# Key spreading on ScalarE, later and smaller query-weight products on GpSimd, and another row for the maxima, in a chain of four cross-attention layers

## The chip, the cores and the metric

The kernel runs on one core of a Trainium2 chip. The metric is the device time of one execution in microseconds. Engines are called by the profile's short names: PE (TensorE matmuls), PEld (its weight loads), DVE (VectorE), ACT (ScalarE), POOL (GpSimd), SP (SyncE, which only issues DMAs here).

## The reference, cut to what matters

Four cross-attention layers follow each other on a residual stream of width 256. The layer called 0 takes the context (4 x 64 tokens) as its latents and x (4 x 256 tokens) as the other side; the output of each layer is the x of the next.

```python
x = _L0_xattn_ref(ctx, x, mask_ik0, q_w, q_b, kv_w, kv_b, out_w, out_b, postnorm_w, mlp_w1, ...)  # 16 heads of 16, then an MLP
x = _L1_xattn_ref(x, ctx, mask_ff0, Wq, bq, Wk, bk, Wv, bv, Wo, bo, gamma, beta)                  # 32 query heads of 8, 8 key heads
x = _L2_xattn_ref(x, ctx, ctx, ...)   # two attentions, 16 heads of 128, one more (bias) key each, then an MLP
x = _L3_xattn_ref(x, ctx, mask_bf1, ...)  # 16 heads of 16, then an MLP

# one attention of layer 2
h = _layer_norm(x, ln_scale, ln_offset)
qh = (h @ wq + bq).reshape(b, q_len, 16, 128)
kh, vh = ctx @ wk + bk, ctx @ wv + bv          # and one bias row each behind them
weights = softmax(einsum('bqhk,bthk->bhqt', qh, kh) / sqrt(128))
x = x + einsum('bhqt,bthk->bqhk', weights, vh).reshape(b, q_len, 2048) @ wo + bo
```

In the text the layers are counted from 0, and the kernel's names carry that number (`kT1`, `kbd3`). "The second layer" of the change's short description is layer 1, "the second half" is the second attention of layer 2.

## The kernel before, in words

The program is written by hand, one instruction stream for each engine, with semaphores between them. An engine runs its stream in the order of the lines. A tile in PSUM comes from a ring (`wide`, three of 1024 columns; `narrow`, two of 512); PE waits for a tile to be drained, and the draining engine waits for it to be full.

*Layer 0* runs in 32 steps over eight groups of (batch, half of the width). Queries and keys are rounded into a high and a low part and stored to DRAM, and come back as `qrow` and `krow`, in which 48 rows hold the parts of one head, at partitions 0 and 64. Row `MASK_ROW` (48) carries the mask. `max_scores0` (L643) computes scores over `MAX_ROW` rows, DVE takes their maxima (L1536), PE turns them (L601), ACT negates them into `maxrow`, and two DMAs on ACT's queue (L1174) put them into row `MAX_ROW` of `qrow`, at partitions 49 and 113. The final scores (L662) then contract over `MAX_ROW + 1` rows, so the maximum is subtracted inside the matmul; row `MAX_ROW` of `krow` holds ones, which SP copies at the start from a row of `qrow` that stays one. The rows between are zero in `krow` and one in `qrow` from the memsets at the start.

*The MLPs* (`mlp` on PE, ACT and DVE) work in two halves of 512 tokens. PE makes four "up" tiles for a half (L507), ACT applies the Gelu to each in two instructions of 512 columns (L1142), DVE rounds it (L1440) and subtracts (L1441) for a high and a low part, and the "down" matmuls (L526) take all of them. In the order of PE, the down matmuls of the first half stand behind the first up tile of the second half. They run over six of the eight hidden chunks for two token blocks first and then wait for the rest.

*Layer 1* needs its keys as a block diagonal: `spread_keys(1, kT1, kbd1, head8, 16)` on POOL multiplies the keys, repeated for 16 heads, by a mask `head8` (one where the partition belongs to the head), in two instructions of 4096 elements per partition (L1782). It stands in POOL's stream behind the folded biases and in front of the wait for the last down tile of layer 0's MLP. PE's first `scores1` waits for `kbd_ready` 2. Layer 3 does the same with `kbd3`, 2 x 2048 elements, while DVE spreads the values into `vpad3` (L1692) and the MLP of layer 2 starts.

*Layer 2* folds queries and keys together. For each attention `precompute2` runs over 16 heads. DVE splits the key and value weights of a head (L1590, `kv_low`, behind ACT's rounded copy L1295), PE multiplies them with the context (L818), ACT evacuates, PE forms `G` with the query weights (L846) and, every second head, the products with the output weights (L859); L826 sums the bias values. The query weights arrive in eight groups of four heads, four for each attention. `multiply_wq(n)` on POOL multiplies a group by the norm's offset into `wprod` (L1765) and by the norm's scale in place (L1766), 1024 elements each; `query_shift(n)` on DVE sums `wprod` (L1617) and adds the bias (L1618); `shift_wq` on ACT adds that to the weights (L1303), waiting for `qshift_ready` at the first head of a group. Of the second attention's groups (4 to 7) POOL does 4 and 5 inside the first attention (steps 4 and 5 of `attend`), and 6 and 7 right behind it; DVE does `query_shift` 4 and 5 in steps 5 and 6, and 6 and 7 at heads 6 and 10 of the second precompute.

In an attention (`attend2`), for each block of 128 tokens PE makes scores (L876), DVE the maxima and sums, ACT the exponentials, POOL divides (`normalize`, L1754), PE turns the probabilities (L557) and applies the values (L898); DVE adds the residual (L1412), which frees PE's narrow tile, and takes the statistics, POOL the reciprocal root (L1732), DVE the normalization (L1392).

Of the kernel before, what the change touches and what calls it, by code (L numbers as in the profile page):

```python
# [19 lines left out]
MASK_ROW, MAX_ROW = 48, 49  # L20
# [80 lines left out]
def build(nc, t, out):  # L101
    ctx = ExitStack()
    with ctx:
# [849 lines left out]
        def _(sp):  # L953
# [55 lines left out]
            for i, lo, hi in ((0, 2 * T, KROW), (0, 0, T), (1, T, KROW)):  # L1009
                k0 = 64 * i + MAX_ROW  # L1010
                sp.dma_start(krow[k0:k0 + 1].rearrange("p a r n -> p (a r) n")[:, :, lo:hi].bitcast(F32),
                             qrow[P - 1:P, 0].rearrange("p r n -> p (r n)")[:, 0:hi - lo].unsqueeze(1).broadcast_to([1, 3 * PAIRS0, hi - lo]).bitcast(F32)
                             ).then_inc(ones_loaded, 16)
# [75 lines left out]
        def _(act):  # L1089
# [37 lines left out]

            def mlp(n, func, b1, turned):
# [4 lines left out]
                for half in range(2):  # L1133
                    for fp in range(NF // 2):
# [13 lines left out]
                        if i == TURN_UP[n]:  # L1148
                            norm_turned(*turned, (1,))

# [215 lines left out]
        def _(dve):  # L1366
# [271 lines left out]
            def precompute2(a):  # L1638
                for h in range(H2):
# [6 lines left out]
                    if a == 0 and 3 <= h < 3 + NQ:  # L1646
                        dve.wait_ge(x2_ready, h - 2)
                        stat(2, h - 3)
                    if h in (6, 10):
                        query_shift(4 * a + h // GROUP + 1)  # L1650
# [11 lines left out]
            def attend2(a, rows_before):  # L1662
                u0 = base["2a" if a == 0 else "2b"]
                for step in range(-3, NQ + 3):
# [4 lines left out]
                    if a == 0 and step in (5, 6):  # L1669
                        query_shift(step - 1)  # L1670
# [39 lines left out]
        def _(pool):  # L1710
# [46 lines left out]
            def multiply_wq(n):  # L1757
# [7 lines left out]
                link(g.tensor_tensor(wprod[:, n % 2], wq, offset, ALU.mult))  # L1765
                g.tensor_tensor(wq, wq, scale, ALU.mult).then_inc(wq_multiplied, 1)  # L1766
# [12 lines left out]
            def spread_keys(layer, kT, kbd, mask, heads_):  # L1779
                pool.wait_ge(*wide.empty(("k", layer)))  # L1780
                for c in range(NC):
                    g.tensor_tensor(kbd[:, c],  # L1782
                                    kT[:, c, :].rearrange("p (b k) -> p b k", b=B).unsqueeze(2).broadcast_to([P, B, heads_, T]),
                                    mask[:].unsqueeze(1).unsqueeze(3).broadcast_to([P, B, heads_, T]), ALU.mult
                                    ).then_inc(kbd_ready, 1)
# [53 lines left out]
            spread_keys(1, kT1, kbd1, head8, 16)  # L1839

# [20 lines left out]
            def between2(a):  # L1861
                def each(step):
# [6 lines left out]
                    if a == 0 and step in (4, 5):  # L1869
                        multiply_wq(step)  # L1870
# [12 lines left out]
            multiply_wq(6)  # L1883
            multiply_wq(7)
# [48 lines left out]
```

## Time and profile before

| | us |
|---|---|
| median of the 3 runs shown | 770.53 |
| lowest, highest | 766.96, 774.74 |
| the profiled execution's own time | 768.64 |
| its span, first to last instruction | 766.9 |
| PE busy in the span | 681.7 |
| DVE busy | 500.1 |
| ACT busy | 350.6 |
| POOL busy | 330.0 |

The profile is of one execution; all rows below are of it. Busy time of PE is not PE at its peak, since matmuls are pipelined and their ends are modelled. The granted clock (PEclk) is a mean over a stretch, 1.00 being the upper one of its two levels (2.4 GHz) and 0.50 the lower (1.2 GHz); over the whole span it is 0.942. In the timelines neighbouring instructions of one form are merged.

### The profile page before, as it was taken

How to read it: one execution, taken by the hardware profiler on the slowest of the kernel's cores; microseconds unless marked ns; L12 is line 12 of the kernel's file. 1: busy time of each engine (PE TensorE's matmuls, PEld its weight loads, DVE VectorE, ACT ScalarE, POOL GpSimd, SP SyncE). 2: the span in 40 equal slices, each digit the busy share in tenths (PEclk: the TensorE clock that was granted, in tenths of full speed). 3: DMA queues.
4: the chain of work that ended last, by engine and by line, in shares of the span. 5: the costliest groups of instructions: out<-in, count | busy, mean ns of one | idle time of the engine just before them, and what ended most of it. 6: DMA issues, size and time to landing. Idle time of an engine off the chain costs nothing.

```text
span 766.9 us, 11612 instructions
## 1 busy us (share of the span) xinstructions
PE 681.7 (89%) x4260; PEld 484.9 (63%) x4260; DVE 500.1 (65%) x844; ACT 350.6 (46%) x931; POOL 330.0 (43%) x288
## 2 busy tenths in 40 slices
PE   8789989998898798689999988999997998787798
PEld 6565556456793454467746766774675896345688
DVE  4446567557649999657556785445587874697543
ACT  2144444344114777456657434655661412585311
POOL 5033264533806989475225553003446222485100
PEclk9868899699999999899999999999998999996899
DMA  6955576000006000063330002230000003000000
GB/s 190 247 146 149 160 184 152 2 2 27 1 1 219 1 1 1 1 198 106 111 109 1 1 0 81 85 110 1 2 0 1 1 1 109 1 1 0 1 28 28
DMA packets 41009, 47.23 MB, mean 62 GB/s; under 512 B 5793, under 2 KB 35066, under 8 KB 40954
## 3 DMA queue, kind: packets, MB, share of 16 engines
q1 hardware_dynamic: 39784, 45.47, 19.9%
q10 hardware_dynamic: 1170, 1.02, 0.6%
q8 instruction: 35, 0.57, 0.3%
q14 instruction: 20, 0.16, 0.1%
HBM read 38.24 MB, written 8.13 MB: 60 GB/s over the span
## 4 chain that ended last, share of the span: by engine, by line
PE 57%; DVE 28%; ACT 4%; issue 4%; POOL 4%; DMA 3%; ACTq 0%; SPq 0%; DVEq 0%; POOLq 0%
PE narrow_ps L526 8%; PE wide_ps L876 6%; PE wide_ps L818 6%; PE wide_ps L507 5%; PE narrow_ps L707 4%; PE wide_ps L859 4%; PE narrow_ps L898 4%; DVE mx L1460 3%; DVE scoresb L1456 3%; PE wide_ps L846 3%; PE wide_ps L557 2%; DVE sums L1480 2%; DVE xn L1392 2%; PE wide_ps L643 2%; DVE hidden L1441 2%
## 5 line engine op out<-in xcount | busy, mean ns | idle before, releaser
L1732 POOL TENSOR_TENSOR rstd<-veps,mhalf 128x1 f32<-128x1 f32 x56 | 33.1, 591 | 161.9 <-DVE veps L1384 155.8
L1754 POOL TENSOR_TENSOR probs<-scoresb,rcp 128x1024 f32<-128x1024 f32 x40 | 78.8, 1969 | 28.3 <-DVE rcp L1485 28.3
L1096 ACT ACTIVATE probsT<-wide_ps 128x1024 f32<-128x1024 f32 x40 | 41.1, 1027 | 71.8 <-PE wide_ps L557 71.8
L526 PE MATMUL narrow_ps<-wstream_r,hidden 128*128 128x256 f32 x576 | 71.1, 284 | 2.8 <-DVE hidden L1441 2.5
L526 PEld LDWEIGHTS narrow_ps<-wstream_r,hidden 128*128 128x128 f32 x576 | 70.4, 191 | 3.8 <-DVE hidden L1441 2.7
L507 PE MATMUL wide_ps<-xq_r,wstream_r 128*128 128x512 f32 x192 | 64.0, 416 | 8.3 <-issue 8.0
L557 PEld LDWEIGHTS wide_ps<-ident,probs 128*128 128x128 f32 x320 | 39.8, 152 | 47.8 <-issue 47.4
L557 PE MATMUL wide_ps<-ident,probs 128*128 128x128 f32 x320 | 46.5, 294 | 26.2 <-POOL probs L1754 26.2
L1536 DVE TENSOR_REDUCE mx<-wide_ps 128x2 f32<-128x640 f32 x64 | 49.4, 817 | 27.4 <-PE wide_ps L643 27.2
L818 PE MATMUL wide_ps<-scoresb_r,probs_r 128*128 128x256 f32 x256 | 54.4, 295 | 8.2 <-DVE wstream_r L1590 5.8
L1728 POOL TENSOR_TENSOR xB<-xB,rows 128x256 f32<-128x256 f32 x40 | 30.2, 764 | 72.9 <-DVE rows L1659 72.2
L1142 ACT ACTIVATE scoresb<-wide_ps,col 128x512 f32<-128x512 f32 x48 | 30.4, 685 | 66.8 <-PE wide_ps L507 66.8
L898 PE MATMUL narrow_ps<-region,probsT 128*128 128x256 f32 x256 | 57.8, 380 | 1.6 <-DVE xB L1412 1.6
L876 PE MATMUL wide_ps<-region,actT 128*128 128x512 f32 x128 | 57.3, 595 | 1.4 <-ACT scoresb L1222 1.4
L818 PEld LDWEIGHTS wide_ps<-scoresb_r,probs_r 128*128 128x128 f32 x256 | 41.7, 189 | 18.9 <-issue 12.6
L898 PEld LDWEIGHTS narrow_ps<-region,probsT 128*128 128x128 f32 x256 | 47.5, 190 | 7.7 <-DVE xB L1412 1.8
L1590 DVE TENSOR_TENSOR wstream_r<-wstream,probs_r 128x256 fp32r<-128x256 f32 x64 | 32.7, 555 | 29.9 <-ACT probs_r L1295 29.9
L507 PEld LDWEIGHTS wide_ps<-xq_r,wstream_r 128*128 128x128 f32 x192 | 37.9, 202 | 17.1 <-issue 9.6
L1745 POOL TENSOR_TENSOR scoresb<-scoresb,mx 128x768 f32<-128x768 f32 x24 | 36.8, 1534 | 26.6 <-DVE negmx L1461 26.4
L1222 ACT ACTIVATE scoresb<-wide_ps,negmx 128x64 f32<-128x64 f32 x128 | 39.1, 334 | 12.7 <-DVE negmx L1471 12.5
L1412 DVE TENSOR_TENSOR xB<-narrow_ps,xB 128x256 f32<-128x256 f32 x48 | 20.1, 419 | 35.8 <-PE narrow_ps L526 23.6
L876 PEld LDWEIGHTS wide_ps<-region,actT 128*128 128x128 f32 x128 | 23.8, 190 | 28.9 <-issue 23.9
(195 smaller groups left out, 1599.2 us busy)
## 6 DMA issues: line engine op xcount, KB each, us to landing
wstream<-in_L_xattn_wk SPq DMA_DIRECT2D x8, 512.0 KB, 3.9
wstream<-in_L_xattn_wv SPq DMA_DIRECT2D x8, 512.0 KB, 5.0
wstream<-in_L_xattn_wo SPq DMA_DIRECT2D x8, 512.0 KB, 4.1
qrow<-qscratch SPq DMA_DIRECT2D x16, 192.0 KB
xq<-in_wqT SPq DMA_DIRECT2D x6, 512.0 KB, 5.2
kscratch<-kparts SPq DMA_DIRECT2D x8, 320.0 KB, 2.5
qscratch<-qparts SPq DMA_DIRECT2D x8, 256.0 KB, 3.5
wstream<-in_L_xattn_mlp_w SPq DMA_DIRECT2D x4, 512.0 KB, 4.4
```

What stands on the lines that cost most here:

```text
L507: m = mm(ps[:, j * 512:(j + 1) * 512], w1[pw][:, kc, f * P:(f + 1) * P], xparts[px][:, kc, half * 512:(half + 1) * 512], start=kc == 0 and ...
L526: m = mm(ps[:, 0:D], hidden[:, ph, f, qoff((q + i) % 4)], w2[pw][:, f, :], start=f == 0 and part == 0, stop=f == NF - 1 and part == 2)
L557: m = nc.tensor.transpose(ps[:, j * P:(j + 1) * P], probs[:, u % 2, j * P:(j + 1) * P], ident[:])
L818: last = mm(ps[:, m * 256:(m + 1) * 256], w[:, m, kc, :], cparts[:, part, kc, :], start=kc == 0 and i == 0, stop=kc == NC - 1 and i == 2)
L876: m = mm(ps[:, g * 512:(g + 1) * 512], actT[:, c, qoff(q)], G[:, c, 8 * g:8 * g + 8, b * T:(b + 1) * T], start=c == 0, stop=c == NC - 1)
L898: m = mm(ps[:, 0:D], probsT[:, u % 2, r * P:(r + 1) * P], VW[:, q // 2, r, :], start=r == 0, stop=r == 7)
L1096: nc.scalar.activation(dst, src, ACT.Identity, **kw).then_inc(ring.drained[ring.slot(key)], 1)
L1222: ins = nc.scalar.activation(scoresb[:, u % 3, h * T:(h + 1) * T], wide_ps[:, wide.slot(key), h * T:(h + 1) * T], ACT.Exp, scale=SCALE2, b ...
L1536: v.tensor_reduce(mx0[:, half % 2, qh, pl:pl + 3:2], ps[:, :, 0:KEYS0], AX, ALU.max).then_inc(wide.drained[wide.slot(key)], 1)
L1732: g.tensor_tensor(rstd[:, q:q + 1], veps[:, q:q + 1], mhalf[:], ALU.pow).then_inc(rstd_ready, 1)
L1745: g.tensor_tensor(s3[:, DIRECT:], s3[:, DIRECT:], mx[:, u % 3, DIRECT:].unsqueeze(2).broadcast_to([P, 16 - DIRECT, T]), ALU.subtract).then ...
L1754: g.tensor_tensor(probs[:, u % 2, :].rearrange("p (h k) -> p h k", h=16), s3, rcp[:, u % 3, :].unsqueeze(2).broadcast_to([P, 16, T]), ALU. ...
```

## The change

Four edits are made together.

- The keys of layer 1 are spread by ACT: `spread_keys1(part)` runs in the first MLP behind each of the eight up tiles, and each call issues four ACTIVATEs (Identity with a per-partition scale, a column of `head8`) of 256 elements, one for each (half of the width, head). POOL's `spread_keys(1, ...)` goes. Parts 3 and 7 increment `kbd_ready`.
- `multiply_wq(5)` on POOL moves from step 5 of the first attention to behind it; groups 5, 6 and 7 are multiplied in eight instructions of 256 elements each instead of two of 1024; groups 6 and 7 wait for the tile `G` of heads 1 and 4 of the second precompute. `query_shift(5)` on DVE moves from step 6 of the first attention to head 2 of the second precompute.
- The spreading of layer 3's keys on POOL is done batch by batch, in eight instructions of 512 elements instead of two of 2048.
- `MAX_ROW` is 63 instead of 49, so the two matmuls over these rows contract over 63 and 64 rows, the DMAs write partitions 63 and 127, and the ones are copied from partition 126.

```diff
-MASK_ROW, MAX_ROW = 48, 49
+MASK_ROW, MAX_ROW = 48, 63
...
-                             qrow[P - 1:P, 0].rearrange("p r n -> p (r n)")[:, 0:hi - lo].unsqueeze(1).broadcast_to([1, 3 * PAIRS0, hi - lo]).bitcast(F32)
+                             qrow[P - 2:P - 1, 0].rearrange("p r n -> p (r n)")[:, 0:hi - lo].unsqueeze(1).broadcast_to([1, 3 * PAIRS0, hi - lo]).bitcast(F32)
...
+            def spread_keys1(part):
+
+                if part == 0:
+                    act.wait_ge(wk_ready, NC)
+                for n in range(4 * part, 4 * part + 4):
+                    c, h = divmod(n, 16)
+                    last = nc.scalar.activation(kbd1[:, c, :, h, :], kT1[:, c, :].rearrange("p (b k) -> p b k", b=B),
+                                                ACT.Identity, scale=head8[:, h:h + 1])
+                if part % 4 == 3:
+                    last.then_inc(kbd_ready, 1)
+
             def mlp(n, func, b1, turned):
...
                         if i == TURN_UP[n]:
                             norm_turned(*turned, (1,))
+                        if n == 0:
+                            spread_keys1(i)
...
                     if a == 0 and 3 <= h < 3 + NQ:
                         dve.wait_ge(x2_ready, h - 2)
                         stat(2, h - 3)
+                    if a == 1 and h == 2:
+                        query_shift(5)
...
-                    if a == 0 and step in (5, 6):
-                        query_shift(step - 1)
+                    if a == 0 and step == 5:
+                        query_shift(4)
...
                 wq = wq2[n]
-                link(g.tensor_tensor(wprod[:, n % 2], wq, offset, ALU.mult))
-                g.tensor_tensor(wq, wq, scale, ALU.mult).then_inc(wq_multiplied, 1)
+                size = 1 if n >= 5 else GROUP
+                for h in range(0, GROUP, size):
+                    last = g.tensor_tensor(wprod[:, n % 2, h:h + size], wq[:, h:h + size], offset[:, 0:size], ALU.mult)
+                link(last)
+                for h in range(0, GROUP, size):
+                    last = g.tensor_tensor(wq[:, h:h + size], wq[:, h:h + size], scale[:, 0:size], ALU.mult)
+                last.then_inc(wq_multiplied, 1)
...
                 for c in range(NC):
-                    g.tensor_tensor(kbd[:, c],
-                                    kT[:, c, :].rearrange("p (b k) -> p b k", b=B).unsqueeze(2).broadcast_to([P, B, heads_, T]),
-                                    mask[:].unsqueeze(1).unsqueeze(3).broadcast_to([P, B, heads_, T]), ALU.mult
-                                    ).then_inc(kbd_ready, 1)
+                    for b in range(B):
+                        last = g.tensor_tensor(kbd[:, c, b],
+                                               kT[:, c, b * T:(b + 1) * T].unsqueeze(1).broadcast_to([P, heads_, T]),
+                                               mask[:].unsqueeze(2).broadcast_to([P, heads_, T]), ALU.mult)
+                    last.then_inc(kbd_ready, 1)
...
-            spread_keys(1, kT1, kbd1, head8, 16)
...
-                    if a == 0 and step in (4, 5):
+                    if a == 0 and step == 4:
                         multiply_wq(step)
...
             attend(base["2a"], NQ, 3, done2, None, between2(0), False)
-            multiply_wq(6)
-            multiply_wq(7)
+            for n in range(5, 8):
+                if n > 5:
+                    pool.wait_ge(*wide.full(("G", 1, 3 * n - 17)))
+                multiply_wq(n)
             attend(base["2b"], NQ, 4, done2, "L2_b_fc2", between2(1), False)
```

## Rows read from the trace of the kernel before

**Rows 1.** The page: span of the profiled execution.

```profile
span 766.9 us, 11612 instructions
```

**Rows 2.** DVE timeline, first MLP: start us, us, engine, line, operation, out<-in, forms.

```profile
185.64 1.22 DVE L1441 TENSOR_TENSOR hidden<-scoresb,hidden 128x1024 fp32r<-128x1024 f32 x1
...
193.85 7.97 DVE L1441 TENSOR_TENSOR hidden<-scoresb,hidden 128x1024 fp32r<-128x1024 f32 x1
```

**Rows 3.** Line 1782: instructions, ns least/median/most, first to last start us, forms.

```profile
L1782 POOL TENSOR_TENSOR region<-headbuf,head x2: 7401/7724/8048, 193.3 to 200.7; 128x4096 f32<-128x4096 f32 x2
L1782 POOL TENSOR_TENSOR region<-kT,head x2: 3618/3663/3708, 592.1 to 595.7; 128x2048 f32<-128x2048 f32 x2
```

**Rows 4.** PE timeline, same stage; brackets: idle before it, and the releaser.

```profile
194.91 4.47 PE L526 MATMUL narrow_ps<-wstream_r,hidden 128*128 128x256 f32 x36
201.88 7.52 PE L526 MATMUL narrow_ps<-wstream_r,hidden 128*128 128x256 f32 x60 [2.50 <-DVE hidden L1441]
```

**Rows 5.** ACT timeline, same stage.

```profile
185.57 1.26 ACT L1142 ACTIVATE scoresb<-wide_ps,col 128x512 f32<-128x512 f32 x2 [0.53 <-PE wide_ps L507]
```

**Rows 6.** ACT timeline, start of layer 2's second precompute.

```profile
455.95 0.84 ACT L1096 ACTIVATE headbuf<-wide_ps,col 128x256 f32<-128x256 f32 x2 [6.38 <-PE wide_ps L818]
456.68 0.51 ACT L1303 ACTIVATE xq<-xq,qshift 128x256 f32<-128x256 f32 x1
```

**Rows 7.** POOL timeline, first attention of layer 2 and behind it.

```profile
439.09 2.38 POOL L1765 TENSOR_TENSOR wprod<-xq,rows 128x1024 f32<-128x1024 f32 x1
...
456.88 2.41 POOL L1765 TENSOR_TENSOR wprod<-xq,rows 128x1024 f32<-128x1024 f32 x1
```

**Rows 8.** DVE timeline, same stages.

```profile
439.07 2.55 DVE L1392 TENSOR_SCALAR xn<-xB,mv,rstd 128x256 f32<-128x256 f32 x1
...
446.21 0.40 DVE L1392 TENSOR_SCALAR xn<-xB,mv,rstd 128x256 f32<-128x256 f32 x1
...
456.95 2.49 DVE L1392 TENSOR_SCALAR xn<-xB,mv,rstd 128x256 f32<-128x256 f32 x1 [0.66 <-POOL rstd L1732]
...
462.78 4.52 DVE L1590 TENSOR_TENSOR wstream_r<-wstream,probs_r 128x256 fp32r<-128x256 f32 x2
```

**Rows 9.** PE timeline, same stages.

```profile
442.01 3.72 PE L898 MATMUL narrow_ps<-region,probsT 128*128 128x256 f32 x16 [1.58 <-DVE xB L1412]
446.42 1.06 PE L557 MATMUL wide_ps<-ident,probs 128*128 128x128 f32 x8 [0.69 <-POOL probs L1754]
...
462.41 0.35 PE L818 MATMUL wide_ps<-scoresb_r,probs_r 128*128 128x256 f32 x1 [2.99 <-DVE wstream_r L1590]
```

**Rows 10.** The chain that ended last, second precompute: start us, us, what.

```profile
464.19 1.71 PE wide_ps L846 x4
465.90 1.01 PE narrow_ps L826 x8
...
473.19 0.87 PE wide_ps L846 x4
...
481.59 0.57 PE narrow_ps L826 x8
```

**Rows 11.** Groups of POOL, 385 to 480: busy us, mean ns, idle before.

```profile
L1728 POOL TENSOR_TENSOR xB<-xB,rows 128x256 f32<-128x256 f32 x8 | 5.6, 726 | 18.0 <-DVE rows L1659 18.0
```

**Rows 12.** Line 1692: DVE copies beside the spreading of layer 3's keys.

```profile
L1692 DVE COPY region<-v x8: 218/224/3635, 592.2 to 600.7; 64x128 f32<-64x128 f32 x8
```

**Rows 13.** Line 1609: DVE copies beside the first two groups of query weights.

```profile
L1609 DVE COPY region<-v x16: 186/192/2455, 231.2 to 243.0; 64x64 f32<-64x64 f32 x16
```

**Rows 14.** PE timeline, MLP of layer 2.

```profile
606.73 0.50 PE L507 MATMUL wide_ps<-actT_r,wstream_r 128*128 128x512 f32 x1 [0.15 <-DVE actT_r L1426]
```

**Rows 15.** Stretches of layer 0: busy by engine, PEclk, DMA share, GB/s.

```profile
40.00:60.00 20.00, 17.73 (x80) 12.66 (x78) 9.04 (x13) 6.99 (x15) 5.74 (x5) 0.60 0.54 151
...
140.00:155.00 15.00, 14.61 (x103) 7.09 (x103) 6.67 (x8) 4.61 (x10) 6.38 (x5) 0.56 0.01 2
```

**Rows 16.** Waits, 20 to 165: who waited for whom, us, times, longest.

```profile
PE wide_ps L662 <- DMA qrow<-maxrow: 0.6, 1, 0.6
```

## What the rows make of the change: the prediction

> **What bounds the kernel now.** The profiled execution has a span of 766.9 us [rows 1] and a time of 768.64 us, so 1.74 us lie around the span; the median of the runs shown is 770.53 us, 1.89 above it, and those runs spread from 766.96 to 774.74. I read first the page's chain that ended last, which is mostly TensorE with VectorE in second place, and then the stages in which the change acts: the timelines of POOL, DVE, PE and ACT side by side. What the reader is to see there is one pattern. A DVE instruction that reads and writes SBUF and starts beside a POOL tensor instruction ends when that POOL instruction ends. The MLP's subtraction takes 1.22 us alone, and 7.97 us when it starts half a microsecond behind the first of POOL's two key-spreading instructions of 7.4 to 8.0 us [rows 2, 3]. The normalization L1392 takes 0.40 us alone, 2.55 and 2.49 us beside a `multiply_wq` half of 2.4 us [rows 7, 8]. It matters only where PE then runs dry, and the PE timeline says where.
>
> **The change, part by part.**
>
> *A. Layer 1's keys go from POOL to ACT.* POOL loses 15.4 us in the first MLP [rows 3]. DVE's subtraction then ends near 193.85 + 1.22 = 195.07 instead of 201.82. PE had finished what it could do without it at 194.91 + 4.47 = 199.38 and stood 2.50 us for it [rows 4]. That wait goes, and PE is next limited by its own matmuls: **2.5 us**. What is late next is ACT. It gets 32 ACTIVATEs of 256 elements. A pair of that size takes 0.84 us out of PSUM, one alone in SBUF 0.51 [rows 6], so a group of four costs 1.7 to 2.0 us and eight groups 13.4 to 16.3 us. They sit behind the Gelu pairs of 1.26 us; ACT still waited 0.53 us for PE at the third [rows 5]. Following the order of the lines I get the third pair about 1 us late and the fourth under 0.5, both estimates. The cover is the gap between 195.07 and PE's need at 199.38: 4.3 us. If all three groups in front of the fourth pair stood in the open (6.1 us), 1.8 us of it would reach PE and A would be worth 0.7; nothing in the ACT timeline points there. In the second half of the MLP ACT has nothing but the Gelus. Later, `scores1` waits for `kbd_ready`; ACT's last increment comes with the last Gelu, before the last down matmuls of the MLP, so it costs nothing. POOL's clearing of `region` and its first two `multiply_wq` hang on the end of the MLP as before and move with it.
>
> *B1. `multiply_wq(5)` and `query_shift(5)` leave the first attention.* POOL's two instructions from 439.09 on hold DVE's normalization for 2.55 us where 0.40 is its own [rows 7, 8]. The residual addition behind it frees a PSUM slot that PE waits 1.58 us for, and 4.4 us later PE waits another 0.69 us for POOL's probabilities [rows 9]. Taking the first wait alone gives 1.58, both 2.27. Of the second part stays, since the last `normalize` still needs the last sums: **2.0 us**.
>
> *B2. The same work in pieces, in the second half of the precompute.* Today `multiply_wq(6)` starts at 456.88, 0.07 us before the last normalization, and the four instructions follow each other; behind it are held the normalization (2.49 us) and both pairs of weight splits, the second for 4.52 us [rows 7, 8]. PE stands 2.99 us for the first pair [rows 9], and the matmuls behind that wait run as at the lower clock level: the next four L846 take 1.71 us against 0.87 in a later group, the next eight L826 1.01 against 0.57 [rows 10]. That is 0.84 + 0.44 = 1.28 us on top. After the change POOL runs `multiply_wq(5)` here, eight pieces; a POOL instruction of 256 elements takes 0.73 us [rows 11], so 5.8 us instead of 4.8. It is due only at the fifth head, when ACT wants `qshift_ready` 6, long after. DVE now waits at most 0.73 us per instruction instead of 2.4. From below: normalization and one pair, three instructions, each behind a whole piece, 2.2 us, leave 2.99 - 2.2 = 0.8 us and no clock gain. From above: 2.99 + 1.28 = 4.27 us. I take a value near the upper end, because DVE's chain runs ahead of PE's next need by then, less 0.5 us (an estimate, part of one 0.73 us piece) for `multiply_wq(6)`, which now starts after the second head and meets the split for the fifth: **3.7 us**. `multiply_wq(7)` starts after the fifth head and is due at the eleventh; POOL has nothing else to do there, so both cost nothing. `query_shift(5)` becomes two DVE instructions behind the third head; the queue behind them, the next splits, is ahead of PE. No DMA is issued or moved.
>
> *C. Layer 3's keys in eight pieces of 512 instead of two of 2048.* By their own rate a piece takes 3.66 / 4 = 0.92 us [rows 3]; by the 256-wide instruction twice 0.73 = 1.45 [rows 11]. DVE has eight copies beside them, two held 3.6 us, the others 0.22 free [rows 12]. In the stage after the first MLP, where four POOL instructions follow each other, only a few of sixteen copies are held, but each for a whole instruction, up to 2.46 us [rows 13]: pieces that follow without a break pass the block on from copy to copy. Eight copies behind eight pieces end after 7.4 to 11.6 us, against 2 x 3.64 + 6 x 0.22 = 8.6 today. PE's only wait that comes from it is 0.15 us [rows 14]. So the ends are +0.15 and -3.0; I take **0.1 us**, by the instruction's own rate.
>
> *D. The row of the maxima.* Partition 49 becomes 63, and the contractions of L643 and L662 take 63 and 64 rows instead of 49 and 50. The added rows are zeros times ones, and the column counts stay, so no instruction is added: **0**, with two rivals below.
>
> Sum: 2.5 + 2.0 + 3.7 + 0.1 = 8.3 us. Against the profiled execution's own time that is 768.64 - 8.3 = 760.3, against the median 762.2; I say **761**. The bounds of the terms give 0.7 + 1.58 + 0.8 - 3.0 = 0.1 us at worst and 2.5 + 2.27 + 4.27 + 0.15 = 9.2 us at best.
>
> **Rivals.**
>
> *The clock rises in layer 0.* In two stretches of it, 40 to 60 and 140 to 155, the mean granted clock is 0.60 and 0.56 while PE is busy nearly throughout [rows 15]: (1 - 0.60) x 2 x 20 = 16 us and (1 - 0.56) x 2 x 15 = 13.2 us at the lower of the two levels. If the longer contraction lifts half of that to the upper level, (16 + 13.2) / 2 / 2 = 7.3 us go: 753.7; all of it would give 746.4. For it: PE hardly idles there, so something other than idling holds the clock down. Against it: the same instructions run at the upper level in the rest of the layer. Chance 0.24. The Trainium skill (TensorE: Matmul & The Clock Gate, § What's actually happening) has the gate follow how busy PE has recently been, and (§ Architectural detail) the array built from blocks of 32 rows. By these, rows 50 to 64 change nothing and this rival falls; the two stretches, busy and slow together, agree with the first of them only in part, so I keep the rival.
>
> *The pieces hold DVE as long as the whole did.* If the pattern of the sixteen copies rules B2 and C, the low ends hold there: 2.5 + 2.0 + 0.8 - 1.0 = 4.3, with a third of C's loss, instead of 8.3: 765. For it speaks [rows 13]; against it that in B2 DVE has three instructions, not a stream. Chance 0.14.
>
> *Maxima arrive late: slower than before.* Sixteen halves of layer 0 each wait for two small DMAs into the changed row. PE has waited for them once, 0.6 us [rows 16]. If the new row landed later by more than the slack, every half would pay; from 8.3 / 16 = 0.52 us each this eats the whole gain, and 1 us each gives 761 + 16 = 777. Nothing in the profile shows a row that lands later. Chance 0.04. [...]
>
> *It does nothing that can be measured*, because other waits take the place of PE's: 769, chance 0.03.
>
> **How the numbers follow.** The forecast has 0.55, with a range of its own of 757 to 766, the spread of single runs included. For 8 in 10 I add the clock rival below and the pieces rival above: 748 to 769. What a measurement of this kernel can tell from no change is about 1%, 7.7 us, so "faster" means below 762.8: 0.6 of the forecast (0.33) and the clock rival whole (0.24), 0.57 in all. Slower by over 1% is the late maxima and a remainder, 0.05. The rest, 0.38, is within 1%.
>
> **What would show it.** In the profile after: all Gelu-stage subtractions on DVE near 1.2 us and PE's down matmuls of the first MLP unbroken (A); PE's waits of 1.58 and 2.99 us gone and L846 near 0.87 us throughout (B); the eight copies each held about 0.9 us (C); the granted clock of 40 to 60 and 140 to 155 unchanged (D). I am wrong if PE waits for ACT in the first MLP, if the weight splits still hold PE while the pieces run, or if layer 0 ends at another time than before.

## The result, and the profile after

The changed kernel takes 750.55 us (median, 749.88 to 753.39) beside 770.67 us for the kernel before (766.96 to 774.74): a ratio of 0.9745, with a 95% interval of 0.969 to 0.980. The forecast was 761. The gain is 20.1 us where 8.3 were worked out. The measured time lies inside the range (748 to 769) and outside the likeliest case's own (757 to 766). Single executions of 1613 to 2688 us (two of the kernel before, one of a_d_max49) are left out of the ratios below.

The profiled execution of the changed kernel took 749.88 us. First its page, span and instructions (answers to [rows 1]):

```profile
span 748.2 us, 11666 instructions
```

The first MLP in its chain that ended last (start us, us, what). The down matmuls come in two unbroken groups of 96; before, the first of them was cut into 36 and 60 by a wait of 2.50 us [rows 4]:

```profile
180.22 7.08 PE wide_ps L507 x24
187.31 11.56 PE narrow_ps L526 x96
198.87 8.19 PE wide_ps L507 x36
207.05 11.59 PE narrow_ps L526 x96
```

The subtractions of that stage on the DVE timeline. None is held as the one of 7.97 us was [rows 2]:

```profile
177.08 1.23 DVE L1454 TENSOR_TENSOR hidden<-scoresb,hidden 128x1024 fp32r<-128x1024 f32 x1
...
186.63 1.23 DVE L1454 TENSOR_TENSOR hidden<-scoresb,hidden 128x1024 fp32r<-128x1024 f32 x1
```

PE's waits at the start of the second precompute, where 2.99 us stood before [rows 9] (in brackets the idle time ahead of the row and who ended it):

```profile
446.53 0.36 PE L818 MATMUL wide_ps<-scoresb_r,probs_r 128*128 128x256 f32 x1 [0.26 <-DVE wstream_r L1603]
455.13 0.36 PE L818 MATMUL wide_ps<-scoresb_r,probs_r 128*128 128x256 f32 x1 [1.12 <-DVE wstream_r L1603]
```

Layer 3's copies beside the spreading in pieces (least, median, most ns; first and last start), the answer to [rows 12], and two stretches of layer 0, the answer to [rows 15] (busy us by engine, then granted clock, DMA share, GB/s):

```profile
L1707 DVE COPY region<-v x8: 962/975/1058, 575.8 to 583.0; 64x128 f32<-64x128 f32 x8
```

```profile
40.00:60.00 20.00, 18.53 (x83) 13.38 (x83) 8.77 (x14) 7.47 (x15) 5.32 (x5) 0.57 0.53 136
...
140.00:155.00 15.00, 14.04 (x148) 7.89 (x146) 8.60 (x14) 9.35 (x18) 5.69 (x5) 1.00 0.01 3
```

The second stretch is the surprise. Before, its granted clock was 0.56, most of it at the lower of the two levels (1.2 GHz); here it is 1.00, the upper one (2.4 GHz) throughout. Layer 0 ends 8.6 us earlier than in the profile before (first L507 of the MLP at 166.14 against 174.72 us), though only step D touches it.

From such chain rows I cut fourteen profiles into the same stages; this table is worked out from them, one execution a line, in us. "Layer 0" is the start of the first L507 of the first MLP; "MLP" goes from there to the end of the second L526 x96; "layer 1" from there to layer 2's first L818 of the chain; "layer 2" to the first L876 of its second attention; "C" on to the L526 of its MLP; "rest" to the end.

| kernel | layer 0 | MLP | layer 1 | layer 2 | C | rest | span |
|---|---|---|---|---|---|---|---|
| before | 174.72 | 54.46 | 101.61 | 189.81 | 88.69 | 157.61 | 766.9 |
| before_again | 166.24 | 63.19 | 102.61 | 189.81 | 88.71 | 158.34 | 768.9 |
| after | 166.14 | 52.50 | 101.63 | 183.93 | 88.05 | 155.95 | 748.2 |
| after_again | 166.18 | 52.46 | 100.71 | 183.92 | 88.30 | 158.93 | 750.5 |
| d_alone | 165.33 | 63.12 | 102.71 | 189.73 | 88.72 | 158.39 | 768.0 |
| row49_k64 | 169.27 | 63.08 | 102.99 | 189.59 | 88.72 | 158.35 | 772.0 |
| d_max49 | 171.96 | 54.42 | 100.85 | 189.81 | 88.71 | 157.55 | 763.3 |
| no_d | 168.06 | 52.52 | 102.35 | 183.96 | 88.05 | 158.66 | 753.6 |
| a_alone | 168.35 | 52.51 | 101.65 | 189.79 | 88.71 | 157.59 | 758.6 |
| a_alone2 | 176.53 | 52.50 | 102.93 | 189.70 | 88.70 | 158.44 | 768.8 |
| b_alone | 175.01 | 54.44 | 100.79 | 183.87 | 88.71 | 156.78 | 759.6 |
| spread_late | 169.75 | 51.72 | 100.06 | 188.35 | 89.05 | 160.17 | 759.1 |
| spread_pieces | 167.59 | 52.49 | 102.47 | 189.80 | 88.17 | 158.78 | 759.3 |
| wq_steps | 164.52 | 52.48 | 105.10 | 183.93 | 88.09 | 158.58 | 752.7 |

Read the two columns on the left together. The start of the MLP varies by some 10 us from one execution to the next. But in the six profiles in which GpSimd spreads the second layer's keys whole and at its old place (before, before_again, d_alone, row49_k64, d_max49, b_alone), a late start (171.96 and later) goes with an MLP of 54.4 us and an earlier one with 63.1, so that both reach layer 1 at 226 to 232 us. Without it the MLP takes 52.5 us (51.7 in spread_late) at any start, 176.53 included, and an early start is kept. "Layer 2" falls by 5.9 us wherever B is in, "C" by 0.4 to 0.6 wherever the pieces of step C are.

### The profile page after: what moved, and what is told of

It is laid out like the page before. It is cut to its first block, busy times and chain, and to the rows that moved or that the text cites. A ratio compares the mean times of both kernels' runs of the same rounds, so it can differ in the third digit from the quotient of the medians.

```text
span 748.2 us, 11666 instructions
## 1 busy us (share of the span) xinstructions
PE 669.0 (89%) x4260; PEld 478.0 (64%) x4260; DVE 488.0 (65%) x844; ACT 363.4 (49%) x963; POOL 319.3 (43%) x310
## 4 chain that ended last, share of the span: by engine, by line
PE 62%; DVE 24%; POOL 4%; ACT 4%; issue 4%; DMA 2%; ACTq 0%; SPq 0%; POOLq 0%; DVEq 0%
PE narrow_ps L526 9%; PE wide_ps L507 8%; PE wide_ps L876 7%; PE narrow_ps L898 6%; PE wide_ps L818 5%; PE narrow_ps L707 4%; PE wide_ps L859 4%; DVE mx L1473 3%; DVE scoresb L1469 3%; PE wide_ps L557 3%; PE wide_ps L846 3%; DVE sums L1493 2%; POOL probs L1769 2%; DVE mx L1549 2%; PE wide_ps L643 2%
## 5 line engine op out<-in xcount | busy, mean ns | idle before, releaser
L507 PE MATMUL wide_ps<-xq_r,wstream_r 128*128 128x512 f32 x192 | 64.3, 418 | 8.0 <-issue 8.0
L526 PE MATMUL narrow_ps<-wstream_r,hidden 128*128 128x256 f32 x576 | 70.9, 284 | 0.3 <-DVE xB L1425 0.3
L526 PEld LDWEIGHTS narrow_ps<-wstream_r,hidden 128*128 128x128 f32 x576 | 70.3, 191 | 1.1 <-DVE xB L1425 0.5
L557 PEld LDWEIGHTS wide_ps<-ident,probs 128*128 128x128 f32 x320 | 38.2, 148 | 48.2 <-issue 47.8
L557 PE MATMUL wide_ps<-ident,probs 128*128 128x128 f32 x320 | 45.0, 287 | 26.3 <-POOL probs L1769 26.3
L818 PE MATMUL wide_ps<-scoresb_r,probs_r 128*128 128x256 f32 x256 | 54.2, 295 | 6.5 <-DVE wstream_r L1603 4.2
L876 PE MATMUL wide_ps<-region,actT 128*128 128x512 f32 x128 | 57.3, 595 | 1.4 <-ACT scoresb L1235 1.4
L1743 POOL TENSOR_TENSOR xB<-xB,rows 128x256 f32<-128x256 f32 x40 | 30.3, 766 | 54.4 <-DVE rows L1674 53.8
L818 PEld LDWEIGHTS wide_ps<-scoresb_r,probs_r 128*128 128x128 f32 x256 | 41.6, 189 | 17.1 <-issue 10.5
L1603 DVE TENSOR_TENSOR wstream_r<-wstream,probs_r 128x256 fp32r<-128x256 f32 x64 | 30.7, 523 | 30.3 <-ACT probs_r L1308 30.3
L507 PEld LDWEIGHTS wide_ps<-xq_r,wstream_r 128*128 128x128 f32 x192 | 38.4, 204 | 16.6 <-issue 8.7
L1235 ACT ACTIVATE scoresb<-wide_ps,negmx 128x64 f32<-128x64 f32 x128 | 39.3, 336 | 12.6 <-DVE negmx L1484 12.5
L1425 DVE TENSOR_TENSOR xB<-narrow_ps,xB 128x256 f32<-128x256 f32 x48 | 20.1, 419 | 36.4 <-PE narrow_ps L526 23.6
L507 PE MATMUL wide_ps<-actT_r,wstream_r 128*128 128x512 f32 x96 | 40.4, 421 | 2.3 <-DVE actT_r L1439 2.3
```

The source lines that it names most:

```text
L507: m = mm(ps[:, j * 512:(j + 1) * 512], w1[pw][:, kc, f * P:(f + 1) * P], xparts[px][:, kc, half * 512:(half + 1) * 512], start=kc == 0 and ...
L526: m = mm(ps[:, 0:D], hidden[:, ph, f, qoff((q + i) % 4)], w2[pw][:, f, :], start=f == 0 and part == 0, stop=f == NF - 1 and part == 2)
L557: m = nc.tensor.transpose(ps[:, j * P:(j + 1) * P], probs[:, u % 2, j * P:(j + 1) * P], ident[:])
L818: last = mm(ps[:, m * 256:(m + 1) * 256], w[:, m, kc, :], cparts[:, part, kc, :], start=kc == 0 and i == 0, stop=kc == NC - 1 and i == 2)
L876: m = mm(ps[:, g * 512:(g + 1) * 512], actT[:, c, qoff(q)], G[:, c, 8 * g:8 * g + 8, b * T:(b + 1) * T], start=c == 0, stop=c == NC - 1)
L1235: ins = nc.scalar.activation(scoresb[:, u % 3, h * T:(h + 1) * T], wide_ps[:, wide.slot(key), h * T:(h + 1) * T], ACT.Exp, scale=SCALE2, b ...
```

## The experiments

The edits are shown shortened; `...` and comments stand for what is left out.

**First question: does layer 0's part of the gain come from row 63?** Four kernels on one chip, before 773.42 us there. *d_alone* is the kernel before with step D alone:

```
-MASK_ROW, MAX_ROW = 48, 49
+MASK_ROW, MAX_ROW = 48, 63
```

> The kernel before with only the maxima's row moved from 49 to 63 (step D alone): the score products of layer 0 contract over 63 and 64 rows in place of 49 and 50. Theory 'the rows' (layer 0's part of the gain, 8.6 us of chain by its end in the two profiles, comes from row 63): about 762 us, 8 below before, the end of layer 0's attention near 157 in the profile where before had 165, and no half-clock stretch at 75 to 81 and 139 to 153. Rival 'the phase' (the half-clock stretches fall elsewhere because something small at the start shifted, and D only carried the profile there by chance): 770 plus or minus 3, and stretches that move about. Rival 'the other edits': 770, layer 0 as in before.

Measured: 769.30 us, 0.9946 (0.9913 to 0.998). Its layer 0 does end early, as "the rows" asked for, and yet 8 us don't arrive: the first MLP takes 63.12 us. D alone is not the gain.

*no_d* is the changed kernel with the row put back:

```
-MASK_ROW, MAX_ROW = 48, 63
+MASK_ROW, MAX_ROW = 48, 49
```

> The changed kernel with the maxima's row put back to 49 (step D undone; ScalarE's spreading, the later and smaller query weight products and the keys in pieces kept). Theory 'the rows': 758 to 760, and layer 0 as long as in before (its end near 165). Rival 'the phase' or 'the other edits': about 750, with layer 0 ending near 157.

Measured: 754.32 us, 0.9766 (0.9722 to 0.9809), layer 0 ending early with the row at 49. Nearly the whole gain is there without D. As the explanation of 8.6 us, "the rows" falls. The next two take D's contraction apart:

```
# d_max49: row 63, the maxima's products as before
-  m = mm(ps[...], qrow[k0:k0 + MAX_ROW, ...], krow[k0:k0 + MAX_ROW, ...])
+  m = mm(ps[...], qrow[k0:k0 + 49, ...], krow[k0:k0 + 49, ...])
# row49_k64: row 49, the score products over 64 rows
-  krow[k0:k0 + MAX_ROW + 1, ...], qrow[k0:k0 + MAX_ROW + 1, ...]
+  krow[k0:k0 + 64, ...], qrow[k0:k0 + 64, ...]
```

> Row 63 as in d_alone, but the products that take the maxima (L643) contract over 49 rows as before, and only the score products (L662, x128) over 64. If the gain of row 63 is in the score products: as d_alone, about 762 by the theory 'the rows'. If it takes the maxima's products: between that and 770. Rival 'the phase': 770.

> The kernel before with its row at 49, but the score products L662 contract over 64 rows (rows 50 to 63 hold zeros), so the number of rows is D's and the place of the row is not. Theory 'the rows': as d_max49, about 762. If it is the place that counts, that is what the row's transfers meet: about 770, while d_max49 is near 762. Rival 'the phase': 770.

Measured: 771.16 us, 0.9972 (0.9947 to 0.9997), and 770.10 us, 0.9977 (0.9949 to 1.0006). Neither is near 762. The score products' rows alone (row49_k64) can't be told from nothing, and the interval of d_max49 ends at 0.9997.

**Second question: what lengthens the first MLP when it starts early?** In the table the MLP column takes one of two values. The DVE, POOL and PE timelines of a late and an early execution tell them apart. Late, the kernel before as profiled at first:

```profile
192.86 0.95 DVE L1440 CAST hidden<-scoresb 128x1024 fp32r<-128x1024 f32 x1 [0.41 <-ACT scoresb L1142]
193.34 15.41 POOL L1782 TENSOR_TENSOR region<-headbuf,head 128x4096 f32<-128x4096 f32 x2
...
202.90 0.42 DVE L1412 TENSOR_TENSOR xq<-narrow_ps,xq 128x256 f32<-128x256 f32 x1 [1.08 <-PE narrow_ps L526]
```

Early, the same kernel in before_again:

```profile
184.86 14.53 POOL L1782 TENSOR_TENSOR region<-headbuf,head 128x4096 f32<-128x4096 f32 x2
185.97 6.52 DVE L1440 CAST hidden<-scoresb 128x1024 fp32r<-128x1024 f32 x1 [1.99 <-ACT scoresb L1142]
192.52 7.95 DVE L1441 TENSOR_TENSOR hidden<-scoresb,hidden 128x1024 fp32r<-128x1024 f32 x1
200.53 9.13 PE L526 MATMUL narrow_ps<-wstream_r,hidden 128*128 128x256 f32 x60 [8.87 <-DVE hidden L1441]
```

Late, the cast starts 0.48 us before GpSimd's first product and runs almost free (0.95 us, and 0.68 when nothing else is on); only the subtraction behind it is held, and the second product, from 200.7 on [rows 3], finds nothing on VectorE that it can hold: a residual addition with an input in PSUM takes its usual 0.42 us. Early, the cast starts 1.11 us behind the first product and is held to its end (6.52 us), and the subtraction then starts with the second product and is held for all of that (7.95 us). PE stands 8.87 us instead of 2.50.

GpSimd's start hangs on the MLP's own start: it is 18.62 us behind the first L507 in both (193.34 - 174.72, 184.86 - 166.24), and 18.62 or 18.63 in the other four of the six. The cast is what moves, 18.14 us behind it late and 19.73 early, because in the early execution PE's twelve L507 ahead of the cast take 4.34 us instead of 2.76 (chain that ended last, late and early):

```profile
188.78 2.76 PE wide_ps L507 x12
```

```profile
180.31 4.34 PE wide_ps L507 x12
```

The granted clock over those matmuls says why (same columns as above; first the late execution, then the early one):

```profile
188.00:193.00 5.00, 4.19 (x18) 3.10 (x19) 4.52 (x7) 2.53 (x4) 5.00 (x7) 1.00 0.00 0
```

```profile
180.00:185.00 5.00, 5.00 (x17) 3.99 (x18) 3.91 (x4) 1.60 (x3) 4.92 (x7) 0.66 0.00 0
```

So the theory "the collision": the 1.6 us that these matmuls lose at the lower clock level let GpSimd in ahead of the cast, and that costs 8.7 us. The other four profiles agree: from 14 to 18 us behind the first L507 the granted clock is 1.00 in all three with an MLP of 54.4 us and 0.57 or 0.58 in all three with 63.1. The next four kernels test it, with before at 770.32 us. *before_again* is the kernel before, unchanged:

> The kernel before, unchanged, for a second profile of it. Theory 'the collision': layer 0 ends (first L507) either near 174 with a first MLP and projections of 54.4 us, or between 165 and 170 with 63.1 us, so that both come to 228 to 232. Rival: layer 0 is always late in this kernel, 174 and 54.4 as in the profile at hand.

Measured: 770.60 us, and the early pair of 166.24 and 63.19 us that the rows above are from. The early layer 0 comes without any change. *a_alone* is step A alone:

```
+  def spread_keys1(part): ...    # ScalarE, behind each Gelu pair of the first MLP
-  spread_keys(1, kT1, kbd1, head8, 16)    # GpSimd
```

> The kernel before with step A alone: ScalarE spreads the second layer's keys during the first MLP, GpSimd doesn't. Theory 'the collision': GpSimd's two products of 7.3 us each hold one VectorE instruction to their end; where layer 0 ends late (before's profile) one hold reaches the path, 2.0 us, and where it ends early and the clock is halved in the first MLP, both do, and the first MLP and projections (from the first L507 to the end of the second L526 x96) take 63.1 in place of 54.4 us. Then A takes 2.0 us off some executions of before and 10.6 off the others: 762 to 766, 0.986 to 0.992 of before, and that stretch takes 52.5 us wherever layer 0 ends. Rival 'A is what the sum said': 770.9, 2.5 us less than before, 0.997. Rival 'the edits need each other' (no part alone brings much): 0.995 to 1.0.

Measured: 760.45 us, 0.9873 (0.9832 to 0.9914): 9.9 us from step A alone, where the sum had 2.5. *spread_late* leaves the products on GpSimd and whole, and adds one wait:

```
+  pool.wait_ge(hidden_split, 4)
   spread_keys(1, kT1, kbd1, head8, 16)
```

> The kernel before with one wait added: GpSimd spreads the second layer's keys as before, with the same two products of 7.3 us, but starts when VectorE has done the first half's last subtraction (L1441). Theory 'the collision': nothing long is on VectorE then, so it brings what a_alone brings, within 2 us (762 to 767), and the first MLP and projections take 52 to 54 us. Rival 'GpSimd's time' (the product's length counts, as the keys are needed for the second layer's first scores): not faster than before, 773. Rival 'A is what the sum said': 2 us off at most.

Measured: 758.83 us, 0.9846 (0.9806 to 0.9887). One wait brings what the move to ScalarE brings. GpSimd's work is no shorter for it (14.10 us for the two products, 14.53 and 15.41 above); they only start behind the last subtraction of the first half:

```profile
188.90 1.22 DVE L1441 TENSOR_TENSOR hidden<-scoresb,hidden 128x1024 fp32r<-128x1024 f32 x1
190.26 14.10 POOL L1782 TENSOR_TENSOR region<-headbuf,head 128x4096 f32<-128x4096 f32 x2 [1.94 <-issue]
195.20 0.42 DVE L1412 TENSOR_TENSOR xq<-narrow_ps,xq 128x256 f32<-128x256 f32 x1 [5.07 <-PE narrow_ps L526]
...
202.07 2.84 DVE L1440 CAST hidden<-scoresb 128x1024 fp32r<-128x1024 f32 x1
```

What still meets the products shows which kind is held. The addition with one input in PSUM is not, the cast from SBUF to SBUF is (2.84 us in place of 0.68, about to the second product's end).

*b_alone* is B1 and B2 alone:

```
-  if a == 0 and step in (4, 5): multiply_wq(step)
+  if a == 0 and step == 4: multiply_wq(step)
-  multiply_wq(6); multiply_wq(7)
+  for n in range(5, 8): ... multiply_wq(n)    # in pieces of 256
```

> The kernel before with steps B1 and B2 alone: the fifth query weights product leaves the second layer's first attention, and products 5 to 7 run in pieces of 256. Theory: 5.9 us off, as in the pair of profiles (between 395 and 512 us), 767.5, 0.992 to 0.993; the first MLP as in before, 54.4 or 63.1 us from L507 to the end of the second L526 x96. Rival 'half of it is lost again' where pieces hold VectorE as long as the whole did: 2 us off, 0.997.

Measured: 766.50 us, 0.9936 (0.9908 to 0.9964): 3.8 us by the medians, with 5.9 inside the interval, and 5.94 us less in the "layer 2" stage. The profiled execution (span 759.6 us) is the fastest of its twelve, so its span says little; the stage does, for it is 183.9 us in every profile with B and 189.6 to 189.8 in every one without, spread_late (188.35) apart.

**Third: does a hold last as long as one GpSimd instruction, and is there another collision to take away?** Before 773.64 us. *spread_pieces* is step C's edit on the kernel before, where it takes the second layer's keys too:

```
-  g.tensor_tensor(kbd[:, c], ...)
+  for b in range(B):
+      last = g.tensor_tensor(kbd[:, c, b], ...)
```

> The kernel before with step C's edit to GpSimd's spreading alone, which there also takes the second layer's keys: each product of 4096 elements becomes four, so eight of some 1.8 us in the first MLP, still on GpSimd and at the same place. Theory 'the collision' with a hold that lasts as long as one GpSimd instruction: a held VectorE instruction now waits 1.8 us at most, so that the first MLP and projections take 53 to 56 us wherever layer 0 ends, and the time is 761 to 765 (0.988 to 0.993). Rival 'GpSimd's work slows VectorE as long as it lasts', in whatever pieces: 770, 63 or 54 us as in before.

Measured: 762.23 us, 0.9866 (0.9825 to 0.9907). Eight products in a row on GpSimd take 16.38 us, longer than the two, at the same place; the pair that was held 6.52 and 7.95 us now takes 1.33 and 2.81:

```profile
186.21 16.38 POOL L1783 TENSOR_TENSOR region<-headbuf,head 128x1024 f32<-128x1024 f32 x8
187.33 1.33 DVE L1440 CAST hidden<-scoresb 128x1024 fp32r<-128x1024 f32 x1 [2.01 <-ACT scoresb L1142]
188.69 2.81 DVE L1441 TENSOR_TENSOR hidden<-scoresb,hidden 128x1024 fp32r<-128x1024 f32 x1
```

So it is the length of one instruction, not of GpSimd's work. *after_again* and *no_d2* are the changed kernel and no_d once more:

> The changed kernel again, for more of its runs and a second profile: 0.975 of before, the first MLP and projections 52.5 us. Theory 'the collision': where layer 0 ends late here (172 to 175), the run ends some 8 us later, since nothing gives it back.

> no_d again (the changed kernel with the row at 49), beside the changed kernel itself, for what step D is worth there. If row 63 lifts the clock in layer 0: 3 to 4 us slower than after_again. If D is worth nothing: the same within 2 us.

Measured: 752.88 us, 0.975 (0.970 to 0.980), and 754.63 us, 0.977 (0.9725 to 0.9815): 1.75 us apart, which these intervals don't separate. *wq_steps* takes the next collision out of the changed kernel, that of [rows 13]:

```
-  for n in range(2): multiply_wq(n)
+  # between the units of layer 1's attention:
+  if 0 <= step < 2 * NQ and step % 2 == 1:
+      multiply_piece(step // 2)    # 256 elements of product 0 or 1, offset and scale
```

> The changed kernel with one more collision taken away: the first two query weight products of the second layer leave the stretch in which VectorE spreads layer 1's values (16 copies L1622, 11.85 us from the first to the last, of which GpSimd's four products of 2.4 us hold four), and run in eight pairs of pieces between the units of layer 1's attention. Theory 'the collision': the copies take some 3 us, so up to 8.8 us off, less what the pieces hold in the attention: 742 to 747. Rival 'GpSimd is the next bound in the attention': 0 to 2 us off, the attention's units longer by what the copies save.

Measured: 753.50 us, 0.9751 (0.9707 to 0.9796), the same as after_again. The copies did what was expected. First the line in the changed kernel, then in wq_steps, and what VectorE did next there:

```profile
L1622 DVE COPY region<-v x16: 186/192/2389, 220.7 to 232.4; 64x64 f32<-64x64 f32 x16
```

```profile
L1622 DVE COPY region<-v x16: 186/190/193, 219.1 to 222.4; 64x64 f32<-64x64 f32 x16
```

```profile
229.61 1.22 DVE L1469 SCALAR_TENSOR_TENSOR scoresb<-wide_ps,mask 128x1024 f32<-128x1024 f32 x1 [7.00 <-PE wide_ps L775]
```

The sixteen copies take 3.50 us in place of 11.85, and then VectorE waits 7.00 us for PE's first scores, which were late all along. The copies were a cover that ended last by 1.4 us only: first L1469 at 13.98 us behind the MLP's end in the changed kernel, at 12.61 here. The attention gives that back: PE's total wait for GpSimd's probabilities there rises from 14.0 to 20.8 us. The rival, that GpSimd is the next bound in the attention, agrees with both, the time and this wait.

**Fourth: what is D worth?** With step A in, what layer 0 gains is no longer eaten. Before 773.16 us.

```
# a_d: step A and step D
# a_alone2: step A, as a_alone
# a_d_max49: as a_d, L643 over 49 rows
# a_warm24: as a_alone, and
-  for i in range(16): nc.tensor.transpose(...)    # ahead of layer 0
+  for i in range(24): nc.tensor.transpose(...)
```

> The kernel before with steps A and D alone, so that the first MLP takes 52.5 us wherever layer 0 ends, and what D does in layer 0 reaches the end. If D lifts layer 0's clock: 4 us less than a_alone2, about 756.5, the first MLP starting at 164 to 167. If the start only varies: as a_alone2, 760, starting at 166 to 175.

> a_alone again (the kernel before with step A alone), beside a_d on the same chip: 760 to 762 by both, the first MLP starting at 166 to 175.

> Steps A and D, but the products that take the maxima (L643) contract over 49 rows, so that only the score products have D's 64. If D's effect is in the maxima's products (of which there are most columns): as a_alone2, 760. If in the score products: as a_d, 756.5. If there is no effect: all three the same.

> Step A alone with 24 instead of 16 transposes ahead of layer 0, while TensorE waits for its first data: work that changes nothing but TensorE's history. If layer 0 depends on the rows: as a_alone2 within 2 us. If any small shift at the start moves it: off by 3 us or more, either way.

Measured: a_d 757.79 us, 0.9804 (0.9778 to 0.983); a_alone2 763.01 us, 0.9872 (0.9833 to 0.9912); a_d_max49 763.42 us over five executions, 0.9874 (0.9841 to 0.9907); a_warm24 760.02 us, 0.9831 (0.9808 to 0.9854). With D the time is 5.2 us lower here, the intervals of a_d and a_alone2 just don't meet, and it goes with the rows of L643, the maxima's products. But eight transposes more ahead of layer 0, which change no product, bring 3.0 us too (their interval and a_alone2's just overlap). The profiles don't settle it. The mean granted clock over layer 0, one execution each, of a_d, of a_alone2 and of a_alone, which is the same kernel as a_alone2:

```profile
20.00:160.00 140.00, 126.25 (x1020) 78.15 (x1024) 85.43 (x139) 57.06 (x112) 54.75 (x53) 0.87 0.53 138
```

```profile
20.00:160.00 140.00, 127.76 (x919) 77.87 (x923) 80.84 (x131) 52.05 (x102) 50.04 (x48) 0.78 0.50 135
```

```profile
20.00:160.00 140.00, 126.09 (x1016) 78.07 (x1020) 85.54 (x139) 57.01 (x112) 54.66 (x53) 0.87 0.52 138
```

PE is busy for the same 126 to 128 us in all three and gets through 1020, 919 and 1016 matmuls in it. The low clock of 0.78 belongs to the slowest of a_alone2's six executions (770.57 us). a_alone has a_d's 0.87 without D, and so has a_warm24; their first MLPs start at 168.35 and 168.16 us, that of a_d at 168.25. What the clock costs in layer 0 is seen here; that D raises it is not.

## Why the prediction was wrong, and where it was right

**A was the step that failed.** The sum took it at 2.5 us, with bounds of 0.7 and 2.5, from "PE stood 2.50 us for it". In the profile that this was read from it would have been worth 54.46 - 52.50 = 2.0 us, or 2.7 beside the 51.72 of spread_late, which like that profile has the upper clock level there. So the mechanism and even the size were right for that one execution. What was wrong was to take one alignment for the price. In three of the six profiles with that spreading whole and at its old place the MLP took 63.1 us, and there A is worth 10.6 us; over the runs of a_alone it is 9.9. The upper bound could have been read from the same timelines: the subtraction is held by the first product [rows 2, 3], the second product of the same length follows it at once, and the cast in front of the subtraction had escaped by 0.48 us. Had it started behind the product, both would be held: 6.5 + 8.0 us less their own 0.7 and 1.2, 12.6 us in all, of which PE hides a part. A margin of half a microsecond asks for that second case. The pattern itself was read a little short: the held subtraction ends 1.1 us behind the first product (201.82 against 193.34 + 7.40 = 200.74), about its own length, so it looks held to the product's end and then run.

That the time lies in the range at all is luck. The range was drawn down to 748 for the rival of the clock, not for A, whose own bounds ended at 2.5.

A's second case also explains the 8.6 us of layer 0 in the two profiles. The kernel before has early layer 0s as well (before_again, 166.24 us), but loses them again in the first MLP. With A they are kept. The pair of profiles showed it as a gain in layer 0, and the prediction had named it as such ("if layer 0 ends at another time than before"); its cause lies one stage later.

A's other points held. ScalarE's groups of four took 1.70 to 1.72 us, at the low end of 1.7 to 2.0, and PE doesn't wait for the Gelus more than before.

**B1 and B2 were right.** 5.7 us were forecast, 5.9 came ("layer 2", 189.81 to 183.93). Cut at the second head's L818 of the second precompute (456.89 us before, 453.70 in b_alone, where layer 2 starts 0.55 us earlier), B1 is 2.6 us against 2.0, and the remaining 3.3 are B2 against 3.7. PE's waits of 1.58, 0.69 and 2.99 us are gone; 0.26 stays and one of 1.12 us is new, the meeting with `multiply_wq(6)` that was put at 0.5. The slow group of L846 [rows 10] is gone: of the 48 into `headbuf` the longest takes 382 ns, where 631 stood before (ns least, median, most; before, then after):

```profile
L846 PE MATMUL wide_ps<-headbuf,xq x48: 377/378/631, 359.4 to 510.9; 128*128 128x256 f32 x48
```

```profile
L846 PE MATMUL wide_ps<-headbuf,xq x48: 377/378/382, 348.9 to 494.5; 128*128 128x256 f32 x48
```

The rival "the pieces hold DVE as long as the whole did" is out for B2.

**C** was put at 0.1 us, by the instruction's own rate of 0.92 us. A piece takes 1.04 us, each of the eight copies is held 0.96 to 1.06 us, as "about 0.9" foresaw. Together they take 8.08 us in the changed kernel and 8.74 before, and the stage gains 0.4 to 0.6 us, more than the wait of 0.15 us that the sum had for it.

**D** was put at 0, and that may be the second thing wrong. The runs with it are faster: 5.2 us beside a_alone2, 4.1 in d_alone, 1.75 in after_again against no_d2, the last within the intervals. In the first pair of profiles the rival "the clock rises in layer 0" seemed to come true, with 8.6 us where it had 7.3. But before_again, with the row at 49, has a granted clock of 1.00 from 140 to 155 too, so that the sign named for D (the clock there unchanged) changes without D. The rival's sentence on the 32-row blocks leaned on the Trainium skill (TensorE: Matmul & The Clock Gate, § Architectural detail) to say that rows 50 to 64 change nothing. The comparison of a_d with a_d_max49, 763.42 to 757.79 us with L643's rows as the only difference, does not agree with what I drew from it. It is left open why: with nothing but TensorE's history changed a_warm24 came out 3.0 us lower (the intervals just overlap), so D may work through a shift of the same kind and not through the rows as such. The rival of late maxima is out: no wait of L662 on a DMA is left in layer 0 of the changed kernel, where one of 0.6 us stood [rows 16].

The sum with the terms as the runs give them: 9.9 (A) + 5.9 (B) + 0.5 (C) + 1.75 to 5.2 (D) = 18 to 21.5 us, beside 20.1 measured. A, B and C measured together, in no_d and no_d2, gave 19.1 and 19.0 us where their three terms make 16.3; the intervals are too wide to say which term is short.

## What to carry to other kernels

When a long instruction on one engine holds short ones on another, its price isn't the wait that one profile shows. Look by how much the instruction in front of or behind the held one escaped, and price the case in which it doesn't; here a margin of half a microsecond was too small. The cheapest cures here were a later start (one wait, 11.5 us) and shorter instructions (11.4), as good as moving the work to another engine (9.9). And a stage that takes one of two lengths can hide what the stage ahead of it gains: take profiles of the same kernel twice before a difference between two kernels is put down to the edit.

## What the runs showed of the hardware that was not expected

- A VectorE instruction that starts beside a GpSimd product waits for that one instruction and not for GpSimd's work: 6.5 and 8.0 us beside products of 7.1 and 7.5 us, 1.3 and 2.8 beside products of 1.9 us. Only some are held: the cast from SBUF to SBUF and the subtraction with two inputs in SBUF, not the addition with one input in PSUM, 0.42 us with and without. The Trainium skill (Advanced Engine Details and Errata, § GPSIMD Details) has GpSimd share a read and a write interface with VectorE, in conflict with instructions of a 2-port mode or with two SBUF inputs. The trace agrees for the subtraction, which has two SBUF inputs and is held, and for the addition, which has one and isn't. The cast has one and is held, which by that sentence makes it a 2-port instruction; no row here shows the mode. In each of these rows the hold lasts to about the end of the running GpSimd instruction.
- In the first MLP PE waits 2.15 to 2.17 us for a normalization, in each of the seventeen profiles that were read, late or early. Over the next 4 us the granted clock is 1.00 in four of them (before, d_max49, b_alone, spread_late) and 0.57 to 0.61 in the thirteen others. In layer 0, from 140 to 155 us, the four had 0.55 to 0.89 and twelve of the thirteen 0.90 to 1.00, so that it looks like one fall of the clock in one of two places; a_alone2, with 0.50 there and 0.60 behind the wait, has both. What decides it wasn't found: the same wait, with the same work ahead of it, does both.
